# A state-space layer and two attention layers on one core: x, the scales and the semaphores' first increments asked for elsewhere in two prologues

## Chip, core and metric

One NeuronCore of a Trainium2 chip runs the whole program. The metric is the device time of one execution in microseconds. Every execution is the same single launch; the inputs lie in HBM.

## What is computed

x has 16 sequences of 512 tokens with 256 values (float32). A condition c (16 x 256) gives six vectors per sequence. Between them stand a selective scan (a state-space layer) and two layers of local attention with a gated MLP. Cut to what matters:

```python
mod = (silu(c) @ wmod).reshape(16, 6, 1, -1)
sa, ca, ga, sb, cb, gb = (mod[:, i] for i in range(6))       # shift, scale, gate; ga, gb: sign * max(abs, 0.25)
h = layernorm(x) * (1 + ca) + sa
x = x + ga * scan_layer(h, W_in, A_log, W_B, W_C, W_dt, b_dt, D, output_gate, W_out)
h = layernorm(x) * (1 + cb) + sb
x = x + gb * stack(h, wqkv, q_scale, k_scale, wo, ln_g, ln_b, w1, b1, w2, b2)
# scan_layer: xz = h @ W_in.T; B, C, dt from its first half; 16 states for each of 512 channels:
#   state = exp(dt * A) * state + dt * B * x_t;   y = sum(C * state);   y = (y + x * D) * silu(z);   out = y @ W_out.T
# stack, twice: h = shift_token(x); q, k, v = h @ wqkv; q, k = l2norm * scale, rotary; attention in windows of 128
#   with one window back; x += o @ wo; h = layernorm(shift_token(x)) * ln_g + ln_b; x += (a * gelu(g)) @ w2 + b2
```

## The kernel before, in words

`build` (at L2026 by the profile) runs two phases one after the other: `mixer_pass`, the scan phase, over the 16 sequences, and `stack_pass`, the second phase, over 32 passes (16 sequences for each of two layers). Between them the rows go through HBM: `stack_dram` holds h for the second phase, stored at L472.

Work on an engine is a program of its own. Blocks (`nc.Block()`) end with all engines meeting; inside a block the engines wait on semaphores. Each `Signal` is a semaphore of which one pass adds a fixed number; it is begun with one increment, so that a wait for "nothing yet" is a wait for 1. DMAs are asked for by SP and, in the prologues, by ScalarE (ACT), and add 16 when they land.

**Scan phase.** Three blocks lie ahead of its main block.
- `setup_weights` (L1896 on). SP asks for the squares, W_in, c, W_dt, W_out, W_B, W_C and, last, `w_mod` (L1899 to L1907). ScalarE asks for five small ones and does silu, sigmoid and exp, each with a table load. TensorE turns the weights (L1938), 20 groups of transposes that DVE copies or splits into an upper and a lower part (L1964, L1967, L1969); waits until all are copied; folds W_dt and W_B, W_C through W_in (L1944, 16 matmuls of 512 columns and 16 of 32); and multiplies the modulation (L1951, 48 matmuls with 16 columns each from `w_mod`). DVE splits the folded weights (L1975, L1977), makes `neg_a` and `picks`, and, when L1951 is done, copies the modulation and makes scales and gates of it (L1982 to L2000).
- A block for DVE alone (L424 to L434): five memsets and four diagonal matrices `skip_mat`.
- `start_signals` (L66 to L73): GpSimd (POOL) increments every semaphore of the phase, some sixty, one after the other.

The main block runs a hand-written order (`MIXER_ORDER`); each engine's `pipeline` takes its own steps from it. For the first sequence that is: `load_x` on SP (L444); `statistics` on ScalarE (L604 to L614): mean, variance and rate per token of `xt`; `normalise_head` (L620, L624) writes `xn`; `turn_input` and `turn_normalised` on TensorE (L498, L505) turn x and xn into two PSUM banks of `a_work` that both use in turn, so the turned xn waits for the copy of the turned x (L596); `modulate_head` (L590), the split into h_upper and h_lower (L636, L735); and the projections (L515). Then, for 32 units per sequence, ScalarE's decays (L702), DVE's scans (L780), GpSimd's products (L833, L840) and TensorE's sums (L564).

**Second phase.** A block of its own starts it (L1163 to L1197): SP asks for the three thirds of `wqkv` (L1169) and the squares (L1170); ScalarE for the rotary tables (L1175) and, in six loads of 64 and 32 KB with rows of 256 and 128 bytes, for q_scale and k_scale spread over the partitions (`scales`, L1178 to L1180); DVE does memsets; GpSimd increments every semaphore, some sixty. In the main block SP begins with `load_hx` of the first pass (L1272, two halves) and goes on to `load_first`: w_1, w_2, the pieces for the second layer, w_o and short vectors. ScalarE begins with a table load and rounds wqkv (L1616), DVE makes the lower part of it (L1841) and then runs its steps, of which the first is `cut_hx` (`cut_parts`, L1677 and L1679): it splits `hx` into hx_upper and hx_lower. TensorE's first products `by_token` (L1338) wait for both. GpSimd begins with `turn_tables` (L1623), which multiplies the tables with the scales and waits for eight loads (`tables_loaded`, 16 * 8); DVE's `times_sin` (L1718) and GpSimd's `times_cos` (L1632) of the first pass need it. The weights' other parts are rounded and cut during the first pass on ScalarE and GpSimd (L1529 to L1536, L1519, L1638 to L1650).

## Time and profile before

| | |
|---|---|
| median of 3 runs | 4488.06 us (4483.64 to 4491.52) |
| profiled execution | 4487.19 us |
| its span | 4485.4 us, 60363 instructions, mean granted clock 0.975 |
| busy | PE 91%, PEld 59%, DVE 82%, ACT 60%, POOL 60% |
| scan phase's first projection | 63.3 us |
| last store of the scan phase | 1867.4 us |
| second phase's first product | 1889.4 us |

The span is that of the instructions of the one core; what lies around it is 1.8 us. In the page's 40 slices of 112 us the first is filled less than those behind it (PE 4 tenths, POOL 1), and the 17th and 18th, in which the phases meet, are 8 and 5 tenths on PE; all others are at 9 or (two of them) 8 and 7. A line number can be that of a helper: L1338 is `by_token` for q, k and v alike. Times in the timeline are counted from the start of the span.

### The profile page before, as it was taken

To read this page: it belongs to the slowest core of one execution; us is meant where nothing else is said; L and a number is where in the kernel's file an instruction comes from. 1 tells how busy PE (TensorE), PEld (TensorE's weight loads), DVE (VectorE), ACT (ScalarE), POOL (GpSimd) and SP (SyncE) were. 2 spreads that over 40 slices of the span, in tenths; PEclk is the share of its full clock that TensorE was granted. 3 is DMA by queue.
4 is the path that set the end of the run, shared out by engine and by line. 5 is a ranking of instruction groups with operands and counts; after the bars stand their busy time and mean duration, and the time that the engine had idled before them with its cause. 6 is when DMAs were issued, how large, how long until landed. Compare 5 with 4: busy or idle time off the path is not lost. (4 is left out here: it accounts for less than half of the span.)

```text
span 4485.4 us, 60363 instructions
## 1 busy us (share of the span) xinstructions
PE 4072.0 (91%) x19614; PEld 2627.8 (59%) x19614; DVE 3675.2 (82%) x6079; ACT 2680.3 (60%) x5830; POOL 2695.4 (60%) x1329
## 2 busy tenths in 40 slices
PE   4899999999999998558999999999999999999997
PEld 3444444444444444236776767777767767777775
DVE  2999999999999999667877777777768777777874
ACT  4777777777777775324555556565645556565654
POOL 1999999999999999443333434343333334343332
PEclk7999999999999999879999999999999999999998
DMA  2333333333333333411000000001020010101000
GB/s 73 108 114 113 118 114 118 113 114 118 115 121 114 113 118 113 136 69 38 15 28 16 16 28 15 29 15 62 15 78 24 24 34 24 34 20 39 20 29 24
DMA packets 118502, 295.05 MB, mean 66 GB/s; under 512 B 21208, under 2 KB 43664, under 8 KB 118192
## 3 DMA queue, kind: packets, MB, share of 16 engines
q1 hardware_dynamic: 114544, 290.37, 19.5%
q8 instruction: 160, 2.62, 0.3%
q10 hardware_dynamic: 3648, 0.83, 0.1%
q14 instruction: 150, 1.23, 0.1%
HBM read 248.52 MB, written 42.64 MB: 65 GB/s over the span
## 5 line engine op out<-in xcount | busy, mean ns | idle before, releaser
L840 POOL TENSOR_TENSOR a_state<-a_state,a_c_wide 128x1024 f32<-128x1024 f32 x512 | 1196.2, 2373 | 32.5 <-DVE a_state L780 32.0
L564 PE MATMUL a_y_sum<-a_state,a_ident 128*128 128x512 f32 x2048 | 942.9, 597 | 2.5 <-POOL a_state L840 2.5
L1657 POOL TENSOR_TENSOR b_scores<-b_scores,b_row_rate 128x1024 f32<-128x1024 f32 (+1 forms) x256 | 426.2, 1681 | 742.6 <-DVE b_row_rate L1768 742.6
L780 DVE TENSOR_TENSOR_SCAN a_state<-a_decay,a_slot 128x1024 f32<-128x1024 f32 x352 | 790.8, 2273 | 3.1
L1632 POOL TENSOR_TENSOR b_by_cos<-b_qk,b_rotary 128x1024 f32<-128x1024 f32 x128 | 309.9, 2421 | 621.6 <-DVE b_qk L1703 621.6
L1338 PE MATMUL b_bank<-b_w_qkv,b_hx_part 128*128 128x512 f32 x2304 | 624.6, 411 | 46.6 <-DVE b_hx_part L1679 26.5
L564 PEld LDWEIGHTS a_y_sum<-a_state,a_ident 128*128 128x128 f32 x2048 | 385.5, 191 | 405.2 <-issue 339.8
L1543 ACT ACTIVATE b_scores<-b_scores,b_row_bias 128x256 f32<-128x256 f32 (+1 forms) x1024 | 478.1, 471 | 198.8 <-DVE b_row_bias L1757 197.2
L702 ACT ACTIVATE a_decay<-a_dt,a_neg_a 128x512 f32<-128x512 f32 x704 | 458.9, 712 | 108.8 <-DVE a_state L780 106.5
L1338 PEld LDWEIGHTS b_bank<-b_w_qkv,b_hx_part 128*128 128x128 f32 x2304 | 418.9, 192 | 165.9 <-DVE b_qk L1703 31.1
L1449 PE MATMUL b_bank<-b_hn_part,b_w 128*128 128x512 f32 x2112 | 508.6, 398 | 7.1 <-DVE b_hn_part L1679 7.1
L1449 PEld LDWEIGHTS b_bank<-b_hn_part,b_w 128*128 128x128 f32 x2112 | 396.1, 189 | 102.7 <-DVE b_hn_part L1679 8.9
L763 DVE TENSOR_TENSOR a_slot<-a_u,a_slot 128x1024 f32<-128x1024 f32 x352 | 417.6, 1214 | 20.7 <-PE a_slot L556 20.0
L833 POOL TENSOR_TENSOR a_state<-a_u,a_b_wide 128x1024 f32<-128x1024 f32 x160 | 375.6, 2370 | 2.2 <-PE a_y_sum L564 1.9
L702 ACT ACTIVATE a_slot<-a_dt,a_neg_a 128x512 f32<-128x512 f32 x320 | 208.1, 682 | 275.6 <-DVE a_state L780 274.8
L780 DVE TENSOR_TENSOR_SCAN a_state<-a_slot,a_state 128x1024 f32<-128x1024 f32 x160 | 356.6, 2269 | 2.9 <-POOL a_state L833 1.6
L1664 POOL TENSOR_TENSOR b_h_part<-b_h,b_h_part 128x512 fp32r<-128x512 f32 x160 | 206.2, 1289 | 249.7 <-ACT b_h_part L1604 249.7
L1751 DVE CUSTOM_DVE_ANT_0 b_scores<-b_bank,b_squares 128x256 f32<-128x256 f32 (+1 forms) x1024 | 338.2, 387 | 0.3 <-issue 0.3
L1823 DVE SCALAR_TENSOR_TENSOR b_h<-b_bank,b_b_1a,b_gelu 128x512 f32<-128x512 f32 x192 | 143.7, 749 | 188.9 <-POOL b_h_part L1664 117.2
L1498 ACT ACTIVATE b_qk_rot<-b_bank 128x512 f32<-128x512 f32 x256 | 142.7, 596 | 254.8 <-PE b_bank L1338 254.1
L556 PE MATMUL a_slot<-a_bc_parts,a_picks 96*128 96x512 bf16 x704 | 212.1, 383 | 81.5 <-DVE a_state L780 80.9
L1470 PE MATMUL b_bank<-b_h_part,b_w 128*128 128x512 f32 x1088 | 285.9, 401 | 0.0
(209 smaller groups left out, 7053.2 us busy)
## 6 DMA issues: line engine op xcount, KB each, us to landing
a_c_wide<-bc_rows SPq DMA_DIRECT2D x256, 512.0 KB, 3.7
a_b_wide<-bc_rows SPq DMA_DIRECT2D x80, 512.0 KB, 4.7
b_hx<-stack_rows SPq DMA_DIRECT2D x64, 256.0 KB, 3.8
b_x_res<-stack_rows SPq DMA_DIRECT2D x32, 512.0 KB, 3.9
a_xt<-in_L_attn_x SPq DMA_DIRECT2D x16, 512.0 KB, 6.1
x_rows<-a_x_t SPq DMA_DIRECT2D x16, 512.0 KB, 5.4
stack_rows<-a_h_t SPq DMA_DIRECT2D x16, 512.0 KB, 5.5
stack_rows<-b_xc SPq DMA_DIRECT2D x16, 512.0 KB, 2.9
```

The costliest lines, as they stand in the source:

```text
L564: last = nc.tensor.matmul(y_sum[dd][:], ident[:], state[state_ring.slot[q]][:, i, :], start=False, stop=(j == GROUPS - 1 and i == GROUP - 1))
L702: last = nc.scalar.activation(to[:, i, :], dt[slot][:, d, :], ACT.Exp, scale=neg_a[:, d, n:n + 1])
L763: nc.vector.tensor_tensor(slots[q % 2][:], u[slot][:, d, :].unsqueeze(1).to_broadcast([P, GROUP, SEQ]), slots[q % 2][:], ALU.mult).then_in ...
L780: nc.vector.tensor_tensor_scan(flat(h), flat(factor), flat(term), 0.0, ALU.mult, ALU.add).then_inc(scan_done.sem, 1)
L833: nc.gpsimd.tensor_tensor(state[state_ring.slot[q]][:], u[slot][:, d, :].unsqueeze(1).to_broadcast([P, GROUP, SEQ]), b_wide[b_ring.slot[k] ...
L840: nc.gpsimd.tensor_tensor(h[:], h[:], c_wide[c_ring.slot[q // 2]][:], ALU.mult).then_inc(cmul_done.sem, 1)
L1338: last = nc.tensor.matmul(psum.tile(name)[:], x[:, c, w * P:(w + 1) * P].bitcast(F32R), weights[:, c, cols:cols + INNER].bitcast(F32R), st ...
L1449: last = nc.tensor.matmul(psum.tile(f"{stem}{m}")[:], weights[:, c, at * P:(at + 1) * P].bitcast(F32R), x[:, c, :].bitcast(F32R), start=(n ...
L1543: e = nc.scalar.activation(scores[w % 2][:, h, lo:hi], scores[w % 2][:, h, lo:hi], ACT.Exp, bias=row_bias[:, w, h:h + 1], accum_out=row_su ...
L1632: nc.gpsimd.tensor_tensor(by_head(by_cos), by_head(qk), for_heads(rotary[:, w, 0], DIM_HEAD), ALU.mult)\
L1657: nc.gpsimd.tensor_tensor(probs, probs, row_rate[:, w, at].unsqueeze(2).to_broadcast([P, 4, hi - lo]), ALU.mult)\
L1751: last = nc.vector.tensor_tensor_reduce(out=scores[w % 2][:, head, lo:hi], in0=psum.tile(f"s{w}_{g}_{h}")[:, at + lo:at + hi], in1=mask[:, ...
```

## The change

Three things are moved in the scan phase's prologue and three in the second's.

Scan phase: `load_x` of the first sequence is asked for at the end of the setup's SP queue, and its `statistics` and `normalise_head` run at the end of the setup's ScalarE program, behind a table load, when DVE has cleared `ln_eps`, `neg_mean` and `token_rate`; in the main block these steps begin with the second sequence. The increments of all semaphores run on GpSimd inside the setup, the memsets and the diagonal matrices on DVE inside it; the two blocks ahead of the main block are gone. In the setup the modulation's matmuls come before the fold and before the wait for all copies, and DVE's work on the modulation before the split of the folded weights. `xt`, `xn` and three small tiles are placed ahead of the setup's tiles, the others behind as before.

Second phase: `load_hx` of the first pass moves to the head of SP's queue in the first block; the six loads of the scales move from ScalarE's first block to the head of its main program; the increments are spread over ScalarE, TensorE and GpSimd, a third each. DVE splits the first hx before the lower part of wqkv.

```diff
@@ scan phase @@
+        setup_weights(nc, inp, banks_all, ..., signals, sems_cleared, (neg_mean, token_rate), load_first_x, first_statistics)
...
-        with nc.Block() as block:
-            @block.vector
-            def _(dve):
-                nc.vector.memset(root[:], -SERIES_ROOT / 4)
...
-                for c in range(INNER_CHUNKS):
-                    nc.vector.tensor_scalar(skip_mat[:, c, :], ident[:], skip_d[:, c:c + 1], None, ALU.mult)
-        start_signals(nc, signals)
...
             def load_x(s, slot, _):
-                wait(sp, x_t_done, s - 1, CHUNKS)
-                wait(sp, xn_done, s - 1, TILES)
-                sp.dma_start(xt[:], inp["L0_attn_x"][s].rearrange("(t p) d -> p t d", p=P)).then_inc(x_loaded.sem, 16)
+                if s > 0:
+                    load_x_of(sp, s)
@@ setup_weights @@
                 sp.dma_start(w_mod[:], inp["L0_wmod"].rearrange("(c p) f -> p c f", p=P)).then_inc(w_mod_loaded, 16)
+                load_first_x(sp)
+
+            @block.gpsimd
+            def _(pool):
+                for signal in signals:
+                    pool.sem_inc(signal.sem, 1)
...
                 nc.scalar.activation(a_log[:], a_log[:], ACT.Exp).then_inc(a_step, 1)
+                nc.scalar.preload_act_table_set(EXP_AND_LN)
+                act.wait_ge(cleared, 1 + len(to_zero))
+                first_statistics(act)
...
+                pe.wait_ge(w_mod_loaded, 16)
+                pe.wait_ge(cond_copied, 1)
+                for f in range(12):
+                    for c in range(CHUNKS):
+                        last = nc.tensor.matmul(banks[6][:, f * BATCH:(f + 1) * BATCH], w_mod[:, c, f * P:(f + 1) * P],
+                                                cond_t[:, c, :], start=(c == 0), stop=(c == CHUNKS - 1))
+                last.then_inc(mod_full, 1)
                 pe.wait_ge(copied, len(turns))
...
@@ second phase, first block @@
             def _(sp):
+                for c in range(CHUNKS):
+                    sp.dma_start(plain(hx, c), stack_dram[0, :, c, :]).then_inc(hx_loaded.sem, 16)
                 for i, done in enumerate(qkv_loaded):
...
             def _(act):
                 act.dma_start(tables, inp["c_rotary"]).then_inc(tables_loaded, 16)
-                for i, name in enumerate(("L0_ffn_q_scale", "L0_ffn_k_scale")):
-                    rows = inp[name].unsqueeze(0)
-                    act.dma_start(scales[:, :, 0, i, :], rows.to_broadcast([P, DEPTH, DIM_HEAD])).then_inc(tables_loaded, 16)
...
+                for signal in signals[0::3]:
+                    act.sem_inc(signal.sem, 1)
+
+            @block.tensor
+            def _(pe):
+                for signal in signals[1::3]:
+                    pe.sem_inc(signal.sem, 1)
...
             def _(pool):
-                for signal in signals:
+                for signal in signals[2::3]:
                     pool.sem_inc(signal.sem, 1)
@@ second phase, main block @@
-                for c in range(CHUNKS):
-                    sp.dma_start(plain(hx, c), stack_dram[s, :, c, :]).then_inc(hx_loaded.sem, 16)
+                if s > 0:
+                    for c in range(CHUNKS):
+                        sp.dma_start(plain(hx, c), stack_dram[s, :, c, :]).then_inc(hx_loaded.sem, 16)
...
+            half = DIM_HEAD // 2
+            for i, name in enumerate(("L0_ffn_q_scale", "L0_ffn_k_scale")):
+                rows = inp[name].unsqueeze(0)
+                act.dma_start(scales[:, :, 0, i, :], rows.to_broadcast([P, DEPTH, DIM_HEAD])).then_inc(tables_loaded, 16)
...
             nc.scalar.preload_act_table_set(EXP_AND_LN)
...
+            cut_hx_of(0)
             for i in range(len(qkv_loaded)):
```

## Rows read from the trace of the kernel before

**Rows 1.** Part 5 of the page: line, engine, operation | busy us, mean ns | idle before.
```profile
L840 POOL TENSOR_TENSOR a_state<-a_state,a_c_wide 128x1024 f32<-128x1024 f32 x512 | 1196.2, 2373 | 32.5 <-DVE a_state L780 32.0
```

**Rows 2.** Timeline, setup: start us, duration us, engine, line, count [idle before <-releaser].
```profile
5.12 0.47 SPq L1907 DMA_DIRECT2D s_w_mod<-in_L_wmod  x1
...
19.53 8.83 PE L1944 MATMUL a_slot<-s_w_dt_t,s_w_in 128*128 128x512 f32 x16 [0.75 <-DVE s_w_bc_t L1964]
...
28.20 1.87 PE L1944 MATMUL a_slot<-s_w_bc_t,s_w_in 128*128 128x32 f32 x16
...
29.90 7.38 PE L1951 MATMUL a_work<-s_cond_t,s_w_mod 128*128 128x16 f32 x48
...
38.88 0.18 DVE L2000 TENSOR_TENSOR mod<-s_sign,s_size 128x32 f32<-128x32 f32 x1
```

**Rows 3.** SP's own waits up to 60 us: total us, times, longest.
```profile
SPq L69 <- PEq L69: 5.2, 1, 5.2
```

**Rows 4.** Timeline, start of the scan phase's main block, and one row of its second sequence.
```profile
45.94 0.39 SPq L444 DMA_DIRECT2D a_xt<-in_L_attn_x  x1
...
50.45 0.42 ACT L604 ACTIVATE a_xn<-a_xt 128x256 f32<-128x256 f32 x1 [3.22 <-DMA a_xt<-in_L_attn_x]
...
57.96 1.05 ACT L596 ACTIVATE a_x_t<-a_work 128x512 f32<-128x512 f32 x2
...
59.81 0.75 ACT L590 ACTIVATE a_work<-a_work,mod 128x512 f32<-128x512 f32 x1 [0.79 <-PE a_work L505]
...
63.33 6.25 PE L515 MATMUL a_work<-a_h_part,a_w_in_t 128*128 128x512 f32 x18 [2.71 <-DVE a_h_part L735]
...
118.80 0.60 PE L498 MATMUL a_work<-a_ident,a_xt 128*128 128x128 f32 x4
```

**Rows 5.** Timeline, start of the second phase.
```profile
1870.40 2.75 SPq L1169 DMA_DIRECT2D b_probs_t<-in_L_ffn_wqkv  x3
...
1873.19 0.47 SPq L1170 DMA_DIRECT2D b_squares<-in_c_squares  x1
...
1874.88 0.50 ACTq L1180 DMA_DIRECT2D b_rstd<-in_L_ffn_k_scale  x1
1875.79 0.98 SPq L1272 DMA_DIRECT2D b_hx<-stack_rows  x2
1875.80 1.28 ACT L1612 ACT_TABLE_LOAD   x1 [8.47 <-PEq L1163]
...
1877.10 2.00 ACT L1616 ACTIVATE b_w_qkv<-b_probs_t 128x1024 fp32r<-128x1024 f32 x2
1878.18 2.36 DVE L1841 TENSOR_TENSOR b_w_qkv<-b_probs_t,b_w_qkv 128x1024 fp32r<-128x1024 f32 x2 [6.95 <-ACT b_w_qkv L1616]
...
1885.28 0.69 DVE L1677 CAST b_hx_part<-b_hx 128x1024 fp32r<-128x1024 f32 x1 [3.31 <-DMA b_hx<-stack_rows]
...
1885.89 2.34 POOL L1623 TENSOR_TENSOR b_rotary<-b_v,b_rstd 128x1024 f32<-128x1024 f32 x1 [40.13 <-DMA b_rstd<-in_L_ffn_k_scale]
1886.00 3.31 DVE L1679 TENSOR_TENSOR b_hx_part<-b_hx,b_hx_part 128x1024 fp32r<-128x1024 f32 x1
...
1889.37 6.31 PE L1338 MATMUL b_bank<-b_w_qkv,b_hx_part 128*128 128x512 f32 x18 [26.15 <-DVE b_hx_part L1679]
```

**Rows 6.** DMA issues up to 60 us: engine, count, KB, us from issue to landing.
```profile
s_w_mod<-in_L_wmod SPq DMA_DIRECT2D x1, 1536.0 KB, 11.6
```

**Rows 7.** Groups by line, TensorE, from 30 to 33 us and from 34 to 37 us.
```profile
L1951 PE MATMUL a_work<-s_cond_t,s_w_mod 128*128 128x16 f32 x28 | 3.3, 263 | 0.0
...
L1951 PE MATMUL a_work<-s_cond_t,s_w_mod 128*128 128x16 f32 x16 | 3.6, 374 | 0.0
```

**Rows 8.** Busy time by window: PE, PEld, DVE, ACT, POOL, granted clock, DMA share, GB/s.
```profile
34.00:35.00 1.00, 1.00 (x7) 1.00 (x6) 0.00 (x0) 0.00 (x0) 0.00 (x0) 0.50 0.00 0
```

**Rows 9.** Timeline, second phase, first pass and the next pass's split of hx.
```profile
1898.40 3.51 DVE L1718 TENSOR_TENSOR b_qk_rot<-b_qk,b_rotary 128x512 f32<-128x512 f32 x2
...
1979.79 1.23 DVE L1679 TENSOR_TENSOR b_hx_part<-b_hx,b_hx_part 128x1024 fp32r<-128x1024 f32 x1
```

194 lines of the change are left out of this document (101 added, 93 removed).

## The prediction

> **What bounds the kernel now.** The kernel has two long phases, and I read first whether either has slack that a shorter prologue could lose itself in. In the scan phase GpSimd does 512 products of 2373 ns with 32.5 us of idle before all of them together [rows 1], most of it in the first pass: it is back to back to the end, so the scan phase takes as long as its GpSimd queue from the moment that queue starts. The second phase keeps TensorE 90 to 99% busy in the slices of the page. Neither phase looks at a clock: an earlier start is an earlier end. What the change touches is two stretches in which these engines stand: 0 to 63.3 us, before the first projection of the scan phase, and 1867 to 1889.4 us, between the phases. There I followed the timelines and asked in each which instruction ends last.
>
> First stretch: TensorE turns weights until 18.78, waits 0.75 us, folds weights (L1944) from 19.53 to 30.07, multiplies the modulation (L1951) until 37.28, and DVE finishes the modulation at 39.06 [rows 2]. Then nothing but the diagonal matrices and some sixty increments by GpSimd, for which SP waits 5.2 us [rows 3], until x is asked for at 45.94; it is there at 50.45, ScalarE needs until 58.05 for the statistics and the normalised rows, modulates from 59.81, and the first projection starts at 63.33 [rows 4]. Second stretch: the block that starts the second phase runs from 1870.40; SP is through at 1873.66, ScalarE has asked for its last scale at 1875.38, and the next block starts at 1875.80. hx, asked for there, is there at 1885.28, and the first product of phase two starts at 1889.37, when hx is split [rows 5].
>
> **Setup, the modulation moved ahead of the fold.** w_mod is asked for at 5.12 and lands 11.6 us later, at 16.7 [rows 2, 6]; x behind it on the same queue is a third of its size, so neither keeps TensorE from starting L1951 at 18.8. Its price depends on the granted clock. At the higher level 28 of its matmuls have 3.3 us of busy time, 0.118 us each; at the lower, 16 have 3.6 us, 0.225 each [rows 7], and that stretch has a granted clock of 0.50, 1.2 GHz, after TensorE had done nothing but such matmuls for four microseconds at the higher level [rows 8]. TensorE comes to them now from turning, as before from the fold, so the clock should fall again, and sooner, since the turning before it is full of waits for DVE. So I take one microsecond at the higher level (8 matmuls) and 40 x 0.225 = 9.0, less half a microsecond of overlap between neighbours: 9.5, ending at 28.3. Bounds: 48 x 0.118 = 5.7 and 48 x 0.225 = 10.8. The fold then starts at the lower level as it did before: 8.83 + 1.87 [rows 2], with 0.3 for a rise that may come later, 11.0; TensorE ends at 39.3, DVE's last split 0.45 later, 39.8, as it stood from 30.07 to 30.52 before. The modulation's own DVE work (1.7 us) and the four diagonal matrices (0.9 us) lie beside the fold and cost nothing; were TensorE not ahead of them, they would cost 2.6. So setup ends 0.7 us *later* than 39.06. The move pays nothing here by itself: it exchanges 1.7 us of DVE tail for a slower clock.
>
> **Setup, x and the increments.** The increments run on GpSimd from 0.4 us on, some 60 in 5.2 us [rows 3], under the weights' loads; the five memsets on DVE lie before its first work. SP's queue gets one more load after w_mod and nothing is behind it. x lands by about 18.5. ScalarE is free from 12.8, pays a table load of 1.28, and does the 7.6 us of statistics and normalising [rows 4] from 18.5 to about 26, 13 us ahead of the block's end: free. It costs only if x comes after 31. Gone from the path: the block of the diagonal matrices and that of the increments with their barriers. The scan block starts 0.35 us after 39.8, at 40.2, where it was 45.94 [rows 4]: 5.7 us.
>
> **Start of the scan block.** x and its normalised rows are there, so after a table load of 1.28 ScalarE copies the first turned chunk (0.57), TensorE turns the first normalised chunk (0.60 for four transposes at the higher level [rows 4], 1.0 at the lower) and ScalarE modulates: 1.3 + 0.6 + 0.6 or 1.0 + waits of 0.1 each, 2.7 us after the block's start. Before, it was 59.81 - 45.94 = 13.9. That is 11.2 us. From there to the projection, 3.5 us, nothing changes. First stretch: 5.7 + 11.2 = 16.9 us. Bounds: 15.5 with all at the lower clock and a later rise, 22 with the modulation at 5.7 and a fold that starts at the higher level (6.9 for 8.8).
>
> **Second phase, the first block.** SP issues hx (0.98 [rows 5], moved ahead), three wqkv loads (2.75) and squares (0.47): 4.2 us, 3.0 if the 1.8 us for which SP and ScalarE both stood inside this group goes with the scales. ScalarE has one load and 21 increments, about 2.2 us, TensorE and GpSimd 20 each at 0.087, 1.7 us. SP ends last: the block ends at 1873.6 to 1874.9, say 1874.4, 1.4 us earlier. hx is asked for at 1870.4 to 1871.4 with nothing ahead of it; x, as large as both its halves, took 4.5 us [rows 4], so it is there at 1875 and split by 1877, before ScalarE has a weight. It is off the path.
>
> **Second phase, ScalarE's queue.** The six scale loads now stand *in front of* the table load and the three wqkv roundings on ScalarE, and all that TensorE does waits behind them. Before they took 1870.83 to 1875.38, 4.5 us with the stand of 1.8; six times 0.5 is 3.1. I take 3.9, beside SP's eight w_1 loads: 1878.3. Table load 1.28, first rounding 1.0 [rows 5], DVE's split 1.2: the first product starts at 1882.0 instead of 1889.37, 7.4 us earlier. Bounds: 9 (block out at 1873.6, 3.1 us) and 5 (1874.9, 5.5 us). What was removed is the wait for hx (to 1885.28) and its split of 0.7 + 3.31. What is late next is the scales themselves.
>
> GpSimd makes the rotary table when the last scale is there: 1885.89, 10.5 us after the last was asked for [rows 5], and DVE's first use, L1718, stands at 1898.40, 9.03 us behind the first product [rows 9]. It would now be wanted at 1891.0. Asked for until 1878.3, the scales' packets drain from some 1876.5 on, when the tables are in; they took 10 us for it beside SP's loads, so about 1887.5, and the table is ready at 1889.9, one microsecond in hand. I take off 0.2 for it. The w_1 loads are asked for 1.4 us earlier and no longer have hx in front; ScalarE wants them 7 us earlier than before; the last is asked for by about 1881 and, at x's 4.5 us from issue to landing with as much again for the traffic, in by 1890, which is when ScalarE wants it. The chain after that, to 1975, waits on DVE, TensorE and GpSimd in turn and moves as a whole. Second stretch: 7.2 us.
>
> A row and a rule on this. The split of hx took 3.31 us at 1886.00 while GpSimd made the rotary table beside it, and 1.23 us at 1979.79 with GpSimd idle [rows 5, 9]. The Trainium skill, GPSIMD Engine Reference, section 1 (Specifications), says that GpSimd shares its SBUF interfaces with VectorE and contends with DVE instructions that have two SBUF inputs; the trace agrees. By that rule the early split runs undisturbed; the sum above does not need it, since the split is off the path either way. A rule that speaks against the change: the Trainium skill, DMA: Bandwidth & Descriptors, section "Issuing engines are not separate DMA queues", says that the loads of ScalarE and SP run on the same 16 DMA engines and interleave. By it the scales, asked for 3 us later among w_1 and w_2, arrive later than their issue alone says; that is the second rival.
>
> **Sum.** 16.9 + 7.2 = 24.1 us. The profiled execution took 4487.19 us with a span of 4485.4; the median of the runs is 4488.06, 0.9 above it, and I count from the median: 4464.0.
>
> **The rivals.**
> (A) The modulation's matmuls run at the higher clock and the fold after them too: setup ends at 34 to 35, 5 us more, 4459. Against it: the same matmuls lost the clock before 34 [rows 8]. 8%.
> (B) The rotary table is late. The scales' small packets take turns with w_1, w_2 and the spare loads; if the last lands at 1892 the table is ready at 1894.4, 3.4 us after DVE wants it, and GpSimd's work then lies beside DVE's two-input instructions, which take two to three times as long: 5 us back, 4469. For it: 10.5 us for 256 KB before. Against it: their draining began when the tables were in, not when they were issued. 12%.
> (C) The scan phase takes the head start back (its first passes wait for something that did not move): then only 7 us remain, 4481. Against it [rows 1]: GpSimd has no idle time to fill. 5%.
> (D) On the other side: the tiles x, xn and the small ones are now placed ahead of the setup's, so each later tile of the scan phase lies elsewhere. If GpSimd's 672 long products (512 and 160) became slower for it, 24.1 / 672 = 36 ns each eats the gain and 49 ns (2%) makes the kernel slower by 0.2%; at 50 ns it is 4464 + 34 = 4498. Against it: both groups have the same mean within 3 ns on different tiles. 3%.
> (E) The change doesn't do what it says: the statistics end the setup because x lands after 31. For each microsecond after that one is lost; at 37 it is 4470. 2%.
>
> **How the numbers follow.** The forecast has 70%. Its own bounds: 15.5 + 5 = 20.5 and 22 + 9 = 31, 4457 to 4467.5, and the runs before lay 8 us apart. With (A) and (B) and 3 us of spread on either side the range is 4454 to 4473. What a measurement can tell from no change is 0.2%, 9 us, a limit of 4479: faster are the forecast, A, B and E, 0.92; within, (C), 0.05; slower, (D), 0.03.
>
> **What would show it.** In the profile after: L1951's matmuls begin near 18.8 and end near 28, the granted clock beside them at 0.50; x lands before 20 and ScalarE's statistics end by 27; the scan block starts near 40 and the first projection near 46.5. The first product of phase two starts some 7 us earlier when counted from the last h2 store, with a wait on DVE's split of wqkv and not of hx. GpSimd's mean for the state products stays at 2370 ns. It is wrong if the setup ends much before 38 or after 42, if DVE waits for GpSimd's rotary table, or if the time from the first projection to the last store of the scan phase changes by more than 2 us.

## The result, and the profile after

| | before | changed |
|---|---|---|
| median, first comparison | 4489.32 us (5 runs) | 4467.59 us (5 runs, 4462.4 to 4471.25), ratio 0.9950 [0.9937, 0.9963] |
| median, repeated in a later group | 4486.61 us (15 runs) | 4469.45 us (5 runs, 4461.2 to 4470.68), ratio 0.9956 [0.9943, 0.9968] |
| profiled execution, its span | 4487.19, 4485.4 us | 4467.59, 4465.8 us |
| first projection | 63.33 | 45.11 |
| last store of the scan phase | 1867.36 | 1851.30 |
| first product of phase two | 1889.37 | 1867.58 |

The change is worth 17 to 22 us by the medians (20 and 22 by the ratios); the forecast was 24.1 and 4464.0, 3.6 us from the median. One row of part 5 of the page of the changed kernel (line, engine, operation | busy us, mean ns | idle before) answers to [rows 1]:

```profile
L839 POOL TENSOR_TENSOR a_state<-a_state,a_c_wide 128x1024 f32<-128x1024 f32 x512 | 1195.5, 2367 | 31.9 <-DVE a_state L779 31.4
```

2367 ns for 2373 and the same idle: the products pay nothing for their tiles' new places, and the scan phase still goes by GpSimd's queue.

The timeline of the changed kernel from the setup to the first projection (start us, duration us, engine, line; L1966 is the modulation, L1973 the fold, L358 and L378 the first statistic and the normalising, L535 the projections) answers to [rows 2] and [rows 4]:

```profile
5.98 0.62 SPq L350 DMA_DIRECT2D a_xt<-in_L_attn_x  x1
...
18.82 8.90 PE L1966 MATMUL a_work<-s_cond_t,s_w_mod 128*128 128x16 f32 x48
18.99 0.42 ACT L358 ACTIVATE a_xn<-a_xt 128x256 f32<-128x256 f32 x1 [5.10 <-DMA a_xt<-in_L_attn_x]
...
24.52 2.07 ACT L378 ACTIVATE a_xn<-a_xt,a_token_shift,a_token_rate 128x256 f32<-128x256 f32 x4
...
27.56 8.70 PE L1973 MATMUL a_slot<-s_w_dt_t,s_w_in 128*128 128x512 f32 x16
...
36.09 1.87 PE L1973 MATMUL a_slot<-s_w_bc_t,s_w_in 128*128 128x32 f32 x16
...
38.22 0.19 DVE L2029 TENSOR_TENSOR a_w_bc_in<-a_slot,a_w_bc_in 128x32 fp32r<-128x32 f32 x1
38.68 1.28 ACT L721 ACT_TABLE_LOAD   x1 [12.09 <-PEq L1909]
...
38.72 1.07 PE L518 MATMUL a_work<-a_ident,a_xt 128*128 128x128 f32 x8 [0.77 <-PEq L1909]
...
40.72 1.69 PE L525 MATMUL a_work<-a_ident,a_xn 128*128 128x128 f32 x8 [0.93 <-ACT a_x_t L616]
41.59 0.75 ACT L610 ACTIVATE a_work<-a_work,mod 128x512 f32<-128x512 f32 x1 [0.53 <-PE a_work L525]
```

x is there at 18.99 and normalised at 26.6, 12 us before the block wants it. ScalarE's idle of 12.09 us ahead of the main block is that reserve. The block starts 0.3 us after DVE's last split, and its first modulation stands 2.9 us behind its start instead of 13.9.

The start of phase two in the same kernel (L1166 hx, L1169 wqkv, L1617 to L1619 the six scale loads, L1624 the roundings, L1685 and L1687 the split of hx, L1854 the lower part of wqkv, L1340 the products, L1631 the rotary table, L1730 its first use on DVE; L1708 is a small DVE step ahead of that use), beside [rows 5] and [rows 9]:

```profile
1851.30 0.32 SPq L492 DMA_DIRECT2D stack_rows<-a_h_t  x1
1854.34 0.80 SPq L1166 DMA_DIRECT2D b_hx<-stack_rows  x2
...
1855.18 3.29 SPq L1169 DMA_DIRECT2D b_probs_t<-in_L_ffn_wqkv  x3
...
1859.39 0.41 ACTq L1617 DMA_DIRECT2D b_rstd<-in_L_ffn_q_scale  x1
...
1860.36 0.69 DVE L1685 CAST b_hx_part<-b_hx 128x1024 fp32r<-128x1024 f32 x1 [5.19 <-DMA b_hx<-stack_rows]
...
1861.09 1.23 DVE L1687 TENSOR_TENSOR b_hx_part<-b_hx,b_hx_part 128x1024 fp32r<-128x1024 f32 x1
...
1863.06 0.73 ACTq L1619 DMA_DIRECT2D b_rstd<-in_L_ffn_k_scale  x1
1863.83 1.28 ACT L1620 ACT_TABLE_LOAD   x1 [12.55 <-issue]
...
1865.12 2.95 ACT L1624 ACTIVATE b_w_qkv<-b_probs_t 128x1024 fp32r<-128x1024 f32 x3
1866.21 3.50 DVE L1854 TENSOR_TENSOR b_w_qkv<-b_probs_t,b_w_qkv 128x1024 fp32r<-128x1024 f32 x3 [3.89 <-ACT b_w_qkv L1624]
1867.58 5.76 PE L1340 MATMUL b_bank<-b_w_qkv,b_hx_part 128*128 128x512 f32 x18 [20.43 <-DVE b_w_qkv L1854]
...
1872.74 2.35 POOL L1631 TENSOR_TENSOR b_rotary<-b_v,b_rstd 128x1024 f32<-128x1024 f32 x1 [43.05 <-DMA b_rstd<-in_L_ffn_k_scale]
...
1873.88 1.24 DVE L1708 TENSOR_SCALAR b_qk_rate<-b_qk_rate 128x16 f32<-128x16 f32 x1
...
1877.13 3.50 DVE L1730 TENSOR_TENSOR b_qk_rot<-b_qk,b_rotary 128x512 f32<-128x512 f32 x2
```

TensorE now waits for DVE's lower part of wqkv and, behind that, for ScalarE, whose queue was busy with loads until 1863.79. hx was split 1.5 us before ScalarE was free. From the last store to the first product it is 16.3 us instead of 22.0.

**Where the 19.6 us of the two profiled spans went**, by stage, positive for a gain: start to first projection 18.2; first projection to GpSimd's first product -2.5 (22.67 to 25.21 us); from there to the last store 0.4; store to first product of phase two 5.7; from there to the end -2.2. The first and the fourth are what the prediction sums; the second and the fifth aren't in it, and the experiments had to say whether the change or the execution makes them. For the fifth the table below answers: the seven executions with the second phase exactly as changed take 2595.2 to 2598.2 us from the first product to the end, 2596.8 in the mean, the two with the old one 2596.0 and 2596.5. So most of the -2.2 is the one execution; half a microsecond could be the change's.

### The profile page after: what moved, and what is told of

It is laid out like the page before. It is cut to its first block and busy times, and to the rows that moved or that the text cites. A ratio compares the mean times of both kernels' runs of the same rounds, so it can differ in the third digit from the quotient of the medians.

```text
span 4465.8 us, 60343 instructions
## 1 busy us (share of the span) xinstructions
PE 4079.0 (91%) x19614; PEld 2633.1 (59%) x19614; DVE 3674.5 (82%) x6079; ACT 2680.8 (60%) x5831; POOL 2695.4 (60%) x1329
## 3 DMA queue, kind: packets, MB, share of 16 engines
q1 hardware_dynamic: 114544, 290.37, 19.6%
q14 instruction: 150, 1.23, 0.1%
## 5 line engine op out<-in xcount | busy, mean ns | idle before, releaser
L839 POOL TENSOR_TENSOR a_state<-a_state,a_c_wide 128x1024 f32<-128x1024 f32 x512 | 1195.5, 2367 | 31.9 <-DVE a_state L779 31.4
L1340 PE MATMUL b_bank<-b_w_qkv,b_hx_part 128*128 128x512 f32 x2304 | 626.0, 412 | 42.0 <-DVE b_w_qkv L1854 20.4
L1340 PEld LDWEIGHTS b_bank<-b_w_qkv,b_hx_part 128*128 128x128 f32 x2304 | 419.6, 192 | 161.3 <-issue 46.7
```

What stands on the lines that cost most here:

```text
L839: nc.gpsimd.tensor_tensor(h[:], h[:], c_wide[c_ring.slot[q // 2]][:], ALU.mult).then_inc(cmul_done.sem, 1)
L1340: last = nc.tensor.matmul(psum.tile(name)[:], x[:, c, w * P:(w + 1) * P].bitcast(F32R), weights[:, c, cols:cols + INNER].bitcast(F32R), st ...
```

## Experiments

Twelve more kernels, three of them repeats, were timed or profiled in three groups, each on one chip beside the kernel before (4488.8, 4484.97 and 4486.61 us). Each row of the table is one execution, and GpSimd's first product is its first operation behind the first projection. Marks from their timelines, in us:

| kernel | first projection | to GpSimd's first product | from there to last store | store to first product | first product to end |
|---|---|---|---|---|---|
| before | 63.33 | 22.67 | 1781.36 | 22.01 | 2596.02 |
| changed | 45.11 | 25.21 | 1780.98 | 16.28 | 2598.22 |
| changed again | 46.65 | 25.18 | 1780.94 | 13.56 | 2597.57 |
| scan part alone | 46.41 | 22.18 | 1780.84 | 21.51 | 2596.46 |
| second part alone | 63.73 | 25.24 | 1782.46 | 15.23 | 2596.53 |
| second part again | 65.64 | 22.34 | 1780.96 | 15.88 | 2595.31 |
| fold first | 49.37 | 22.38 | 1783.78 | 14.95 | 2597.42 |
| scales back | 46.80 | 22.16 | 1786.46 | 13.86 | 2595.13 |
| x in the block | 57.26 | 22.34 | 1781.02 | 13.54 | 2597.61 |
| busy TensorE | 47.19 | 21.12 | 1786.42 | 13.56 | 2595.17 |
| hx late | 45.66 | 25.05 | 1784.16 | 17.21 | 2594.59 |
| two scale loads | 46.91 | 22.41 | 1783.61 | 12.26 | 2596.36 |
| the same again | 46.76 | 23.74 | 1786.50 | 12.20 | 2596.24 |
| two in the first block | 45.36 | 25.15 | 1780.90 | 13.87 | 2597.42 |

**Each half alone.** The scan phase's functions and the setup as changed with the second phase as before. An extract, against the changed kernel; the scale loads, the increments and DVE's order go back in the same way:

```diff
@@ second phase, first block, SP @@
-                for c in range(CHUNKS):
-                    sp.dma_start(plain(hx, c), stack_dram[0, :, c, :]).then_inc(hx_loaded.sem, 16)
```

> The scan phase's part alone; the second phase's first block and main block as before. Theory: the two parts do not touch each other, and what the changed kernel lost between its first projection (18.2 us early) and GpSimd's first operation (15.7 us early) is the granted clock that fell otherwise on the first projections, no wait. So: first projection near 45.1 us, last h2 store near 1851.5, first product of the second phase 22.0 us behind that store as before, total 16 us less than before (15 to 18), near 4473. Rival: the parts interact (the second part's prologue is what starts early only because of the first), then the distance from store to first product is not 22.0. Rival for the lost 2.5 us: a new wait in the scan prologue; then it is lost again in the same place with the same clock or with another.

4469.99 us (4465.18 to 4474.64), ratio 0.9956 [0.9943, 0.9968]: 18.8 us of 4488.8, where 15 to 18 were expected. From the store to the first product of phase two it is 21.5 us, as in the kernel before, so the two parts don't touch. From the first projection to GpSimd's first product it is 22.18 us, so the 2.5 us lost there in the changed kernel are no wait that its code always has.

The other half, `stack_pass` as changed and the rest as before. An extract, against the kernel before:

```diff
@@ second phase, first block, SP @@
+                for c in range(CHUNKS):
+                    sp.dma_start(plain(hx, c), stack_dram[0, :, c, :]).then_inc(hx_loaded.sem, 16)
```

> The second phase's part alone. Theory: the scan phase as before (last h2 store at 1867.4 within 1 us), first product of the second phase 16.3 us behind it where it was 22.0 before, 5.7 us; total 5 to 6 us less than before, near 4483.5. My recorded sum had 7.2 us for it. Rival: nothing comes out of it alone, because the rotary table, late by the scales, gives it back in the first pass: then the first score product (2nd phase, 108 us behind the store before) is not 5 us earlier.

4485.42 us (11 runs, 4478.12 to 4488.34), ratio 0.9992 [0.9983, 1.0001], 3.4 us by the medians, which the interval doesn't tell from nothing. The rival's mark falls: the first score product stands 102.2 us behind the store, 6.2 earlier than in the kernel before. The kernel was timed again in the third group:

> The second phase's part of the change alone, once more. By the traces its new start is worth 6 to 8 us (22 us from the last h2 store to the first product before, 13.5 to 16.3 with it); by its 11 runs of the first group only 3.4 us with an interval of about 4 on either side. Theory (the whole of it reaches the end): ratio 0.9983 to 0.9989 to the kernel before, 5 to 7.5 us less. Rival (half of it is given back in the first pass, which then waits for something else): ratio 0.9990 to 0.9996.

4484.11 us (11 runs, 4478.22 to 4488.05), ratio 0.9991 [0.9983, 1.0000], 2.5 us by the medians and 4.0 by the means. The rival called half of the gain given back in phase two. The table speaks against a place for it: from the store to the first product it is 15.2 and 15.9 us instead of 22.0 and 21.5, and from the first product to the end 2596.5 and 2595.3, where the two kernels with the old start took 2596.0 and 2596.5. So 6 to 7 us are there in both traces and are not taken back behind them: from the store to the end it is 2611.8 and 2611.2 us instead of 2618.0 and 2618.0. The runs are compatible with that (the interval reaches 7.6 us) but their middle, 0.9991, lies in the rival's band, some 3 us lower; this difference stays open. Together the halves give 21 to 23 us by the runs, the whole change 17 to 22: within this noise they add up.

**The order in the setup.** Everything as changed, but modulation and its DVE work behind the fold again:

```diff
-                pe.wait_ge(w_mod_loaded, 16)
-                for f in range(12): ...              # modulation
                 pe.wait_ge(copied, len(turns))
                 ...                                  # fold
+                pe.wait_ge(w_mod_loaded, 16)
+                for f in range(12): ...              # modulation
```

> The changed kernel with the modulation's matmuls, and DVE's work on them, back behind the fold. Theory of the recorded sum: the move pays little, it exchanges 1.7 us of DVE tail for a slower clock of these matmuls. Then setup ends at 39.1 to 39.4 instead of 38.4 and the total is 0.7 to 1 us more, within what the runs can tell. But TensorE then goes into the scan block with the lower clock and no dense work behind it. Rival: the order decides the clock of the first projections; then the first projections take another time (6.3 us for 18 at the level of before, 7.2 in the changed kernel) and GpSimd's first operation moves by more than the setup's end.

4469.85 us (4461.64 to 4470.2), ratio 0.9952 [0.9939, 0.9966]. TensorE's timeline of this kernel (L1966 is the fold here, L1973 the modulation):

```profile
19.67 10.08 PE L1966 MATMUL a_slot<-s_w_dt_t,s_w_in 128*128 128x512 f32 x16 [0.75 <-DVE s_w_bc_t L1991]
...
31.29 9.35 PE L1973 MATMUL a_work<-s_cond_t,s_w_mod 128*128 128x16 f32 x48
42.73 1.94 PE L518 MATMUL a_work<-a_ident,a_xt 128*128 128x128 f32 x8 [2.09 <-PEq L1909]
```

The block starts at 42.7; in the eight kernels with the whole changed setup it is 38.7 to 40.7, mean 39.9. By the runs the two orders can't be told apart. Against this one execution the move is worth 2.9 us, not the -0.7 predicted, but much of that is the execution: its fold took 11.8 us (19.67 to 31.45) where the old order's three other executions had 10.5, with 5.9 us of it at the lower clock instead of 3.4, and its modulation 9.35 us, not the 7.38 of [rows 2]. The 7.38 was one execution's too: with the old setup untouched it was 7.26 and 9.41 us in the two profiles of the second part alone. In those two and in the kernel before, DVE's last work on the modulation ended at 39.4, 41.5 and 39.1 us, mean 40.0; in the eight with the new order DVE's last split ended at 39.6 in the mean. So the move is worth between 0.4 and 2.9 us, and these executions do not settle where.

**Scales back in the first block.** The six loads in ScalarE's first block, where they were; TensorE and GpSimd do the increments, half each:

```diff
@@ first block, ScalarE @@
-                for signal in signals[0::3]:
-                    act.sem_inc(signal.sem, 1)
+                for i, name in enumerate(("L0_ffn_q_scale", "L0_ffn_k_scale")): ...   # six loads
@@ main block, ScalarE @@
-            for i, name in enumerate(("L0_ffn_q_scale", "L0_ffn_k_scale")): ...
```

> The changed kernel with the six scale loads back in ScalarE's first block, and the increments on TensorE and GpSimd, half each. Theory: in the changed kernel the six loads stand 4.4 us in front of ScalarE's roundings, on the path of the first product, while in the first block ScalarE was idle until SP was through. So the first block ends within 0.8 us of where it did (5.0 us behind its start), and the first product comes 12.3 to 13 us behind the last h2 store instead of 16.3, the total 3 to 4 us less, near 4464. The rotary table is then ready before DVE wants it. Rival: the first product is held by the wqkv loads' landing or by hx as well; then it moves by less than 2 us. Rival two: the first block gets longer by what is gained, since ScalarE's and SP's loads stand behind one another there as they did before (1.8 us each).

4461.7 us (4459.16 to 4466.29), ratio 0.9940 [0.9928, 0.9953]. SP's queue in this kernel (store of h, hx, wqkv, squares, the first w_1 load of the main block):

```profile
1855.43 0.32 SPq L492 DMA_DIRECT2D stack_rows<-a_h_t  x1
1858.48 0.80 SPq L1166 DMA_DIRECT2D b_hx<-stack_rows  x2
1859.33 2.65 SPq L1169 DMA_DIRECT2D b_probs_t<-in_L_ffn_wqkv  x3
1862.01 1.36 SPq L1170 DMA_DIRECT2D b_squares<-in_c_squares  x1
1865.07 4.22 SPq L1228 DMA_DIRECT2D b_scores<-in_L_ffn_w  x8
```

The block is 6.6 us long instead of 3.4 to 5.0, since the scales take 5.8 us to ask for beside SP's loads, but nothing stands ahead of ScalarE's roundings any more: first product 13.9 us behind the store, where the changed code has 13.5 to 16.3. It was expected at 12.3 to 13, but the block grew, as rival two said, and ScalarE then waited 0.48 us for the first third of wqkv, which landed 7.5 us behind its issue, and 0.85 and 0.61 us for the others. So the move of the scales is no gain by itself: what it takes out of the block it puts in front of the roundings. By the runs it is rather a loss: this kernel is 27 us below the kernel before by the medians (26 by the means), the most of all those timed here, and the changed one 17 and 22 (20 and 22), though the intervals still overlap. A possible cause, argued and not tested by itself, is the rotary table, which is done 20.5 us behind the store here and 22.6 to 25.0 behind it in the seven kernels with the changed second phase; what it holds up is told below.

**x back in the main block**, all else as changed:

```diff
-                load_first_x(sp)
...
-                first_statistics(act)
...
-                if s > 0:
-                    load_x_of(sp, s)
+                load_x_of(sp, s)
```

> The changed kernel with x's load, statistics and normalising back in the main block; increments, memsets and diagonal matrices stay in the setup. It gives the price of x alone. Theory: setup ends at 38.4 to 39.8 as it does with x; x is asked for 0.35 us later and 17.4 us behind that (63.33 - 45.94) the first projection starts, so near 56.5 instead of 45.1 to 46.8: x is worth about 10.5 us (the recorded sum had 11.2), and the increments with the blocks 5.7. Rival: x in the setup also slows or holds the setup (it lands beside w_mod, ScalarE shares nothing with the others); then the setup ends earlier than 38.4 here.

4473.85 us (one run). The timeline of this kernel, main block (L358 first statistic, L609 first modulation):

```profile
44.38 0.42 ACT L358 ACTIVATE a_xn<-a_xt 128x256 f32<-128x256 f32 x1 [2.40 <-DMA a_xt<-in_L_attn_x]
...
53.74 0.75 ACT L609 ACTIVATE a_work<-a_work,mod 128x512 f32<-128x512 f32 x1 [0.79 <-PE a_work L524]
```

ScalarE waits for x and then 9.4 us pass, from its first statistic on, before it can modulate; the first projection stands at 57.26, against a mean of 46.2 in the eight kernels with x in the setup: 11.0 us, where 11.2 was predicted. That term is settled as far as one execution can, and the rival falls: DVE's last split ended at 40.4, not earlier than 38.4.

**Is GpSimd's late first product a wait or the clock?** TensorE in the changed kernel, and in the second part alone, again (first projection and dt projection; x counts matmuls). First the changed kernel:

```profile
45.11 7.21 PE L535 MATMUL a_work<-a_h_part,a_w_in_t 128*128 128x512 f32 x18 [2.70 <-DVE a_h_part L734]
...
57.69 4.58 PE L535 MATMUL a_work<-a_h_part,a_w_dt_in 128*128 128x512 f32 x12 [2.61 <-DVE a_bc_parts L745]
```

and the second part alone, again, whose scan phase is that of the kernel before:

```profile
65.64 5.89 PE L515 MATMUL a_work<-a_h_part,a_w_in_t 128*128 128x512 f32 x18 [2.71 <-DVE a_h_part L735]
...
76.90 3.03 PE L515 MATMUL a_work<-a_h_part,a_w_dt_in 128*128 128x512 f32 x12 [2.61 <-DVE a_bc_parts L746]
```

The waits are the same to 0.01 us (2.70 and 2.61); what is longer are the matmuls, 7.21 for the 6.25 of the kernel before and 4.58 for its 2.99, together 2.55 us, which is the whole loss. Busy time by window (PE, PEld, DVE, ACT, POOL, then granted clock, DMA share, GB/s) of the changed kernel:

```profile
55.00:60.00 5.00, 2.39 (x7) 1.89 (x7) 1.28 (x2) 1.77 (x3) 0.00 (x0) 0.81 0.62 195
60.00:65.00 5.00, 2.27 (x7) 1.45 (x5) 0.00 (x0) 3.87 (x6) 0.00 (x0) 0.84 0.95 338
```

and of the scan part alone, which has the same code there:

```profile
51.00:56.00 5.00, 3.94 (x18) 2.38 (x16) 0.69 (x1) 2.60 (x5) 0.00 (x0) 1.00 0.06 15
56.00:61.00 5.00, 3.00 (x12) 2.17 (x12) 0.68 (x1) 2.91 (x6) 0.00 (x0) 1.00 0.67 254
```

One more kernel kept TensorE busy on purpose: eight unwanted matmuls (into a bank that the next real one starts afresh) stand ahead of the turned xn and of the first projection.

```diff
+                if isinstance(s, int) and (s, m) == (0, 0):
+                    keep_busy(6)
                 wait(pe, h_cut, s, CHUNKS)
```

> The changed kernel with eight matmuls of 128 x 512 that compute nothing wanted, two ahead of the first turned xn and six ahead of the first projection, where TensorE has nothing to do. Theory: the time from the first projection to GpSimd's first operation is 22.2 to 22.7 us where the granted clock is low for 8.5 to 9 us of it, and 25.2 where it is low for 15, whatever was changed. If the eight keep the higher clock, the low time is under 4 us and that distance 20.5 to 21.5. If the clock is low at 41 us anyway, they take 0.85 us each, hold the first projection back by up to 2.4 us, and the distance stays at 22 or more. Rival (the distance is set by waits of ScalarE and DVE alone, not by the clock): it is 22 to 25 with a low time under 4 us.

4465.28 us (one run): the first projections take 4.70 us instead of 7.21 and the way to GpSimd's first product 21.1 us, in the range expected, with 5.8 us of it at the lower clock where under 4 were expected. But the projection starts at 47.19, 8.3 us behind the block's start instead of 6.4 and later than in any of the eight kernels without them. GpSimd's first product stands at 68.3, hardly before the kernels where the lower clock fell least on this stretch (68.6 to 69.3). One execution shows no gain to speak of.

The changed kernel was profiled again to see whether 25.2 us are its own:

> The changed kernel once more, timed in five rounds beside the three others of this group. Theory (the late first state product of the profiled execution, 25.2 us behind the first projection where four others took 22.2 to 22.4, is where the low granted clock happened to fall): 4465 to 4469 us beside a kernel before of 4487 to 4489, and this profile may as well show 22 to 22.5 us with 8 to 9 us at the low clock. Rival (the changed code has a wait of its own there): 25 us again. From the last h2 store to the first product of the second phase 13.5 to 16.3 us by either.

4469.45 us. It shows 25.18 again, so this run alone would speak for the rival. The table doesn't: with the same code from the first projection on it is 22.2 to 22.4 us in five kernels (scan part alone, fold first, scales back, x in the block, two scale loads), 23.7 in one and 25.1 to 25.2 in four, and with the code of before 22.3, 22.7 and 25.2. Every 25 has 15 us at the lower clock in that stretch, the 23.7 has 12.9 and every 22 has 8.5 to 9. The two profiles of the second part alone, the same code, show both (25.24 and 22.34). It is the clock and can come with either code. Whether the changed code meets it more often (five of its ten above 23 us, against one of three) is not settled by so few.

**hx late.** Its load at its old place, DVE's order as changed:

```diff
@@ first block, SP @@
-                for c in range(CHUNKS):
-                    sp.dma_start(plain(hx, c), stack_dram[0, :, c, :]).then_inc(hx_loaded.sem, 16)
@@ main block, SP @@
-                if s > 0:
-                    for c in range(CHUNKS):
+                for c in range(CHUNKS):
```

> The changed kernel with the first hx asked for in the main block again, still split first on DVE. Theory: hx is the other half of what held the first product; asked for 5 us behind the last store's end, with wqkv, the scales and w_1 around it, it lands some 8 us later, is split 2 us after that, and DVE's lower part of wqkv stands behind it in DVE's order: first product 19 to 21 us behind the last h2 store instead of 15.0 to 16.3. Rival: the early hx is worth nothing, the scales in front of the roundings set the time; then it stays at 15 to 16.5.

4468.77 us (one run). From this kernel's timeline:

```profile
1861.35 0.91 SPq L1271 DMA_DIRECT2D b_hx<-stack_rows  x2
...
1864.60 1.28 ACT L1617 ACT_TABLE_LOAD   x1 [9.75 <-issue]
1865.90 2.95 ACT L1621 ACTIVATE b_w_qkv<-b_probs_t 128x1024 fp32r<-128x1024 f32 x3
...
1868.86 0.69 DVE L1682 CAST b_hx_part<-b_hx 128x1024 fp32r<-128x1024 f32 x1 [10.10 <-DMA b_hx<-stack_rows]
```

DVE waits 10.10 us, to 7.5 us behind the issue of hx, and only then makes the lower part of wqkv: first product 17.2 us behind the store. That is 2.5 us more than the mean of 14.7 of the seven kernels with the changed code. The expectation of 19 to 21 was too high, and so was my picture of what the early hx brings: of the 7 us, 2.5 come from asking early, by this one execution. The other 4.8 us to the kernel before are in the two timelines [rows 5]: the block is 3.4 us long and was 5.4, hx lands 7.5 us behind its issue and took 9.5, and from the begin of its split to the first product it is 3.2 us instead of 4.1, with no rotary table on GpSimd beside it (1.23 us for the second half of the split instead of 3.31). Which of the edits shortens the landing was not tried.

**Two scale loads instead of six.** If ScalarE's queue is what ends last, fewer loads must show. ScalarE asks for the two whole rows; GpSimd copies their halves crosswise ahead of the rotary table:

```diff
-                act.dma_start(scales[:, :, 1, i, 0:half], rows[:, :, half:].to_broadcast([P, DEPTH, half])).then_inc(tables_loaded, 16)
-                act.dma_start(scales[:, :, 1, i, half:], rows[:, :, 0:half].to_broadcast([P, DEPTH, half])).then_inc(tables_loaded, 16)
...
+            pool.wait_ge(tables_loaded, 16 * 4)
+            for to, at in ((slice(0, half), slice(half, DIM_HEAD)), (slice(half, DIM_HEAD), slice(0, half))):
+                nc.gpsimd.tensor_copy(scales[:, :, 1, :, to], scales[:, :, 0, :, at]).then_inc(rotary_done, 1)
```

> The changed kernel with two loads of the scales instead of six (q_scale and k_scale once each; GpSimd, idle then, copies their halves crosswise in two small copies). Theory: on ScalarE the loads in front of the roundings take 0.9 us instead of 3.5 to 4.4, so the first product comes 12.2 to 13.3 us behind the last h2 store (15.0 to 16.3 in the kernels with six), and the rotary table is ready before that of the changed kernel, since two thirds of the small packets are gone. Total 2.5 to 3.5 us less than the changed kernel, 4463 to 4465. Rival: wqkv's landing or the split of hx (over at 10.9 us behind the store) is next and holds it at 14 or more.

4461.85 us (4458.37 to 4468.09), ratio 0.9948 [0.9934, 0.9961]. And again beside the changed kernel:

> Two scale loads in place of six, GpSimd copies the halves crosswise; the same kernel as in the last group. Theory (ScalarE's queue is what the first product waits for, four loads are 2 to 2.9 us of it): 12 to 13.3 us from the last h2 store to the first product and 2 to 3.5 us less than the changed kernel by the median. Rival (the clock moves more than the loads do, the 4461.85 of the last group was luck): within 1.5 us of the changed kernel.

4464.17 us (4462.18 to 4468.22), ratio 0.9950 [0.9938, 0.9963]; the changed kernel there 4469.45. The first product stands 12.3 and 12.2 us behind the store, 2.5 less than the mean with six loads, as expected; by the runs it is 5.3 us faster by the median, 2.5 by the mean of the five, and the intervals overlap. Beside their kernels before, these two stand 23.1 and 22.4 us lower by the medians, the one with the scales back in the first block 27.1, so the best first product is not the fastest kernel by the runs. Last, the two loads in the first block:

```diff
@@ first block, ScalarE @@
+                for i, name in enumerate(("L0_ffn_q_scale", "L0_ffn_k_scale")): ...   # two loads
                 for signal in signals[0::3]:
@@ main block, ScalarE @@
-            for i, name in enumerate(("L0_ffn_q_scale", "L0_ffn_k_scale")): ...
```

> As the kernel with two scale loads, but they stand in ScalarE's first block behind the tables' load, beside SP's three loads of wqkv, so that nothing is asked for on ScalarE's queue ahead of its roundings. Theory (the block is set by SP's queue and has room for 0.9 us on ScalarE): first product 11.4 to 12.3 us behind the last h2 store, 0 to 0.9 us less than with the two loads in the main program, and then a wait for wqkv's landing or for the split of hx, so no further gain from this queue. Rival (SP and ScalarE hold each other up when both ask for loads, as in the kernel before): the block gets 1 to 1.8 us longer and the first product stands at 12.5 to 14 us, no gain or a loss.

4464.67 us (4460.98 to 4470.62), ratio 0.9949 [0.9935, 0.9962]: no better. The timeline of this kernel:

```profile
1854.84 0.46 ACTq L1177 DMA_DIRECT2D b_rstd<-in_L_ffn_q_scale  x1
...
1855.30 1.57 SPq L1169 DMA_DIRECT2D b_probs_t<-in_L_ffn_wqkv  x3
...
1857.89 1.28 ACT L1617 ACT_TABLE_LOAD   x1 [6.51 <-PEq L1162]
...
1862.82 1.06 ACT L1621 ACTIVATE b_w_qkv<-b_probs_t 128x1024 fp32r<-128x1024 f32 x1 [3.65 <-DMA b_probs_t<-in_L_ffn_wqkv]
...
1865.28 6.87 PE L1343 MATMUL b_bank<-b_w_qkv,b_hx_part 128*128 128x512 f32 x18 [18.02 <-DVE b_w_qkv L1855]
```

The block stays short (3.4 us, the rival falls) and ScalarE is ready at 1859.17, but then it waits 3.65 us for wqkv, which lands 7.5 us behind its issue; with the scales in the main program it landed 5.9 and 5.8 behind it, and ScalarE waited 0.9 and 1.0 us for it there too. The theory was right that a landing ends the gain and wrong on when: 13.9 us, not 11.4 to 12.3. With two loads, in either place, the queue of ScalarE is no longer the bound, the landing of the weights is. That the scales' packets ahead of it cost the 1.7 us is argued from these two kernels and the one with the scales back (7.5 us as well), not shown by itself.

## Why the prediction was right, point by point

**The two mechanisms** are as predicted. The gain is the bare prologue: almost nothing in 1800 us of scan phase or 2600 us of second phase takes it back. [rows 1] against its row of after settles rivals C and D: from its first product to the last store it is 1781.4 and 1781.0 us, its product 2373 and 2367 ns.

**The modulation** ran from 18.82 to 27.72, predicted 18.8 to 28.3; the granted clock was 1.00 from 19 to 20, 0.76 in the next microsecond and 0.50 from 21 on, so rival A falls in the way that [rows 8] said. The fold ended at 37.96 (predicted 39.3), the block began at 38.7 (40.2). Over eight kernels the mean is 39.9, so this execution was a lucky one and the estimate good. What was weak is the sentence on the move itself, "pays nothing", -0.7 us. I compared a forecast with one execution in which the old order's modulation was short (7.38 us). By the executions here it pays 0.4 to 2.9 us, for the tail that it covers.

**The scan block's start**: from block to projection 6.4 us, predicted 6.3; x in the setup 11.0, predicted 11.2. First stretch: 16.9 predicted, 18.2 in the two profiled executions, 18.0 between the means (46.2 in eight kernels, 64.2 in three).

**The second phase's first block** was to be 4.0 us long, 3.2 to 4.5, and was 5.04. This is the term that was mis-sized: SP's three wqkv loads took 3.29 us to ask for, although the scales were gone from beside them, where I had bought back part of a stand of 1.8 us. That part of the sum was loose too: 4.2 less 1.8 is 2.4, not 3.0, and the 1.8 is the whole length of one load on ScalarE's queue whose neighbours took some 0.5, so the stand was 1.3. In the changed kernel profiled again they took 1.62 us and the block 3.4:

```profile
1856.66 1.62 SPq L1169 DMA_DIRECT2D b_probs_t<-in_L_ffn_wqkv  x3
...
1859.25 0.41 ACTq L1617 DMA_DIRECT2D b_rstd<-in_L_ffn_q_scale  x1
...
1862.58 1.28 ACT L1620 ACT_TABLE_LOAD   x1 [9.83 <-issue]
...
1866.34 7.03 PE L1340 MATMUL b_bank<-b_w_qkv,b_hx_part 128*128 128x512 f32 x18 [17.71 <-DVE b_w_qkv L1854]
```

So the stand comes and goes without the scales, by execution: 5.7 us gained in one, 8.4 in the other. The six scale loads took 4.4 and 3.3 us (3.9 predicted), hx landed 6.0 and 5.2 us behind its issue (4.5 predicted, from x), still off the path. Second stretch: 7.2 predicted, 7.0 between the means (14.7 in seven kernels, 21.8 in two).

**The rotary table** was ready at 1875.09 and used at 1877.13, 2 us in hand where one was predicted. But DVE's L1708, on the way to that use, took 1.24 us beside the table, 0.17 otherwise, so the use itself came 1.1 us late. The prediction named a wait of DVE for the table as a sign that it is wrong, and three other executions with the same second phase have it (second part alone, fold first, busy TensorE: 0.96, 0.38 and 0.88 us). From the second part alone:

```profile
1894.04 2.39 POOL L1632 TENSOR_TENSOR b_rotary<-b_v,b_rstd 128x1024 f32<-128x1024 f32 x1 [44.22 <-DMA b_rstd<-in_L_ffn_k_scale]
...
1896.55 5.67 DVE L1731 TENSOR_TENSOR b_qk_rot<-b_qk,b_rotary 128x512 f32<-128x512 f32 x2 [0.96 <-POOL b_rotary L1632]
```

In the other three (changed again, second part again, x in the block) L1708 or its like took 1.68, 1.30 and 1.97 us. So in all seven the table holds DVE up, by 0.4 to 1.8 us, and in neither of the two kernels with the old second phase. Rival B's 5 us do not come, but its mechanism does, in small, and the one microsecond in hand was not there. With two scale loads, where the table is done 18.2 to 19.0 us behind the store, nothing of it is left. The last scale was in 9.7 us behind its issue, beside SP's eight w_1 loads. The rule of the Trainium skill, DMA: Bandwidth & Descriptors, "Issuing engines are not separate DMA queues", that the loads of both queues interleave, agrees with this and with the 7.5 us of wqkv in the last experiment; a landing set the time only in part here, by the table and, with two scale loads, by wqkv. The split of hx took 1.23 us with GpSimd idle, 3.31 before, as the rule on the shared SBUF interfaces (the Trainium skill, GPSIMD Engine Reference, section 1) has it.

**What the sum lacked** is a term for the clock. The mark "changes by more than 2 us from the first projection to the last store" was exceeded, 1804.0 to 1806.2, and was set too tight: the second part alone, with the scan code of before, has 1807.7 and 1803.3. In the profiled pair the two stretches sum to 23.9 us, next to the 24.1 predicted, because one is 1.3 over and the other 1.5 under: that closeness is luck. The stage means give 25.0 us for the two stretches; the runs 21.7 and 17 to 20. Some 2 us may go to a scan phase that is on average 1806.9 us in the eight kernels with the changed scan part and 1805.0 in the three without, but a single kernel moves by 7 us there (1803.0 to 1810.2), and that can't be told from chance here.

## What to carry over

Where the phase behind a prologue has an engine without idle time, a microsecond off the prologue is a microsecond off the end, and loads and statistics that wait for nothing belong beside the setup's matmuls. Before an instruction is moved, look which of two resources ends last after it, here a queue's time to ask for loads and then the landing of the largest; fewer loads brought the first product forward where moving all six behind the block didn't. Follow the chain past the first product as well: the table that the same loads feed was the next thing late. A term that is the difference of one trace's duration and an estimate should be held against how the same group varies: three profiles with the old setup show 7.4, 7.3 and 9.4 us.

## What the runs showed of the hardware

- **Asking for a load has no fixed price.** The same three loads of wqkv took 1.41 (hx late) to 3.29 us on SP's queue, the same six scale loads 3.2 (hx late) to 5.8 us (scales back) on ScalarE's. Between the shortest and the longest start of phase two with the same code lie 2.7 us.
- **GpSimd holds up a small VectorE instruction too.** DVE's L1708, one input of 128x16, has a mean of 183 ns over its 128 instances; beside GpSimd's rotary table it took 1.24 us in the changed kernel and 1.68 when it was profiled again, and 1.30 and 1.97 in two more, each time ending within 0.05 us of the table's end (1875.12 and 1875.09; 1875.40 and 1875.36 in the first two). In the kernel with two loads in the first block, where the table is done earlier, it took 0.17. The section of the Trainium skill named above (GPSIMD Engine Reference, section 1) has the same contention for VectorE's two-port modes; that this instruction runs in one isn't shown here.
- **Which of the two starts first decides who waits.** DVE's two `times_sin` (L1730, two inputs each) took 3.50 us where GpSimd's `times_cos` began 0.14 us behind them (changed kernel) and 5.67 to 5.70 where it began 0.03 us ahead (the three executions that waited for the table). DVE's next step then took 1.23 us instead of 3.20, so the two together are 6.7 us in the one case and 6.9 in the other.
- **The clock is a per-execution cost of some microseconds.** Short stretches at the lower level made the same dt projections last 3.0 or 5.5 us with the same code (the two profiles of the second part alone), and the scan phase's time at the lower clock behind GpSimd's first product varied from 40 us (seven kernels at 1780.8 to 1781.4 us) to 56 us (three kernels at 1786.4 to 1786.5). A difference of 5 us between two traces of this kernel needs a look at the granted clock before it gets another cause.
